# Graph network layer: which engine tells TensorE that a gathered slot is full, and who is told that it was read

## The reference

```
x  = layernorm(x + gcn(x, W, b) + t_emb @ Wt + bt)      # layer 0
h  = relu(mean_over_edges(x[src]) @ Wl1.T + x @ Wr1.T + b1)   # layer 1
y  = mean_over_edges(h[src]) @ Wl2.T + h @ Wr2.T + b2         # layer 2
out = layernorm(x + y)
# gcn: sum over edges of x[src] scaled by 1/sqrt(degree) on both sides, then @ W
# mean_over_edges: segment_sum(msg, dst) / max(count, 1)
```

## Time and profile before

| | |
|---|---|
| three runs | 3864.66, 3865.3 (median), 3870.44 us |
| the profiled execution | 3868.88 us, span of its trace 3867.1 us |
| PE busy | 3067.6 us (79%) |
| POOL busy | 2257.4 us (58%) |
| DVE busy | 1094.8 us (28%) |
| ACT busy | 503.1 us (13%) |
| mean granted clock of TensorE | 0.916 |
| moved by DMA | 1102.52 MB, 285 GB/s over the span |

### The profile page before, as it was taken

One profiled execution on the slowest core, in us unless ns is written; L12 is line 12 of the kernel. 1 busy time (PEld: TensorE's weight loads), 2 busy tenths in 40 slices (PEclk: granted clock), 3 DMA queues, 4 the chain that ended last, 5 costly groups with the idle time before them and its releaser, 6 DMA issues.

```text
span 3867.1 us, 52767 instructions
## 1 busy us (share of the span) xinstructions
PE 3067.6 (79%) x11711; PEld 1400.9 (36%) x12104; DVE 1094.8 (28%) x1877; ACT 503.1 (13%) x1048; POOL 2257.4 (58%) x2367
## 2 busy tenths in 40 slices
PE   7156667778888878788989978886778889988888
PEld 7012223333333333333444433342334344433333
DVE  8701112222333431112222323332122222222222
ACT  0500000111112220000111111111000111111112
POOL 0066666666666636666666666654666666666663
PEclk9988878888899989899999989998889999999999
DMA  5587788888999968888889999987888888888785
GB/s 170 218 301 273 267 274 289 297 305 308 321 323 324 328 244 286 279 282 277 298 309 309 319 328 321 318 311 262 282 278 284 272 281 278 285 280 280 270 279 192
DMA packets 278572, 1102.52 MB, mean 285 GB/s; under 512 B 53626, under 2 KB 55196, under 8 KB 278514
## 3 DMA queue, kind: packets, MB, share of 16 engines
q0 software_dynamic: 187680, 922.63, 69.3%
q10 hardware_dynamic: 64638, 137.22, 10.0%
q1 hardware_dynamic: 26228, 42.34, 3.1%
HBM read 1003.75 MB, written 99.06 MB: 285 GB/s over the span
## 4 chain that ended last, share of the span: by engine, by line
PE 44%; another core or an unknown queue 20%; issue 19%; ACTq 6%; DVE 3%; ACT 3%; DMA 3%; POOL 2%; DVEq 0%; SPq 0%; POOLq 0%
PE sum_ps L1187 27%; PE root_ps L1195 8%; PE prod_ps L1195 7%; POOL raw L457 2%; DMA raw<-table,idx_ring 1%; ACTq L249 1%; PE selfT_ps L1209 1%; PE aggT_ps L1173 1%; ACT selfT L931 1%; ACTq L969 1%; DMA table<-stage 1%; DVE left_of L643 1%; DVE stage L635 1%; ACTq L272 1%
## 5 line engine op out<-in xcount | busy, mean ns | idle before, releaser
L457 POOL DMA_INDIRECT raw<-table,idx_ring x2346 | 2248.0, 958 | 1483.8 <-issue 834.8
L1187 PE MATMUL sum_ps<-raw,oh 128*128 128x512 bf16 x6682 | 1718.1, 402 | 516.4 <-issue 463.6
L1187 PEld LDWEIGHTS sum_ps<-raw,oh 128*128 128x128 bf16 x7038 | 696.1, 102 | 1434.3 <-issue 778.6
L765 DVE TENSOR_TENSOR oh<-iota_ps,dst_rel 128x1280 bf16<-128x1280 f32 x237 | 352.9, 1489 | 1438.5 <-remote 684.2
L1195 PE MATMUL prod_ps<-W,aggT 128*128 128x512 f32 x1176 | 547.4, 607 | 20.9 <-issue 11.8
L1195 PE MATMUL root_ps<-W,selfT 128*128 128x512 f32 x800 | 400.6, 644 | 72.3 <-issue 69.1
L1195 PEld LDWEIGHTS prod_ps<-W,aggT 128*128 128x128 f32 x1176 | 230.3, 197 | 265.9 <-issue 247.4
L887 ACT ACTIVATE aggT<-aggT_ps 128x512 f32<-128x512 f32 x147 | 87.7, 597 | 1827.0 <-remote 1359.9
L1187 PE MATMUL sum_ps<-raw,oh_next 128*128 128x512 bf16 x847 | 229.8, 401 | 37.7 <-issue 26.8
L1195 PEld LDWEIGHTS root_ps<-W,selfT 128*128 128x128 f32 x800 | 160.6, 206 | 270.2 <-issue 258.9
L924 ACT ACTIVATE selfT<-selfT_ps 128x512 f32<-128x512 f32 x100 | 59.7, 597 | 1004.3 <-remote 644.6
(11 more groups left out here) (149 smaller groups left out, 1156.5 us busy)
## 6 DMA issues: line engine op xcount, KB each, us to landing
raw<-table,idx_ring POOLq DMA_INDIRECT x2346
table<-planes ACTq DMA_DIRECT2D x89, 384.0 KB
selfbuf<-rows ACTq DMA_DIRECT2D x104, 256.0 KB
selfbuf<-table ACTq DMA_DIRECT2D x50, 384.0 KB
table<-stage SPq DMA_DIRECT2D x7, 2688.0 KB, 8.3
rows<-X ACTq DMA_DIRECT2D x49, 256.0 KB
X<-rows ACTq DMA_DIRECT2D x49, 256.0 KB
X<-in_x SPq DMA_DIRECT2D x6, 2048.0 KB
```

The source lines that it names most:

```text
L457: nc.gpsimd.indirect_dma_start(out=raw[:, n, j, :], out_offset=None, in_=tables[L][:, :], in_offset=bass.IndirectOffsetOnAxis(ap=idx_ring[ ...
L765: v.tensor_tensor(oh[:, which * HR:(which + 1) * HR, :, :].rearrange("p n j e -> p (n j) e"), iota_ps[:, 0:P].unsqueeze(1).to_broadcast([P ...
L1187: last = mm(bank, of[:, j, :], raw[:, n, j, p * D:(p + 1) * D], start=fresh, stop=False, skip_group_check=True)
```

## The change

`gathered`, `pe_done` and SP's relay are gone. PE waits for `slot_full[n]` itself. In place of `pe_done` there are ten semaphores `slot_read[n]`, one for each slot, each raised by the last matmul on that slot; POOL waits for its slot's, DVE for that of the last slot of the half block. `oh_made` now counts half blocks, and PE waits for it in slots 0 and 5 alone. ACT's wait before it copies row numbers is for `slot_read[9]` (the tenth slot of the block was read) where it was for `gathered` (it has landed). With the relay gone, SP's three later loads stand right behind each other, each with the wait that it had.

```diff
+        slot_read = [sem(f"slot_read{n}") for n in range(SLOTS)]
+        def fills(n, L):
+            return L * (NBLK + (n == 0))
...
-                def landed(blk, n):
-                    fills = NBLK + 1 if n == 0 else NBLK
-                    sp.wait_ge(slot_full[n], blk * (16 * CH) + 16 * CH * (fills * L + 1))
-                    sp.sem_inc(S["gathered"], 1)
-                with sp.Fori(0, ROOTS_DONE) as blk:
-                    for n in range(SLOTS):
-                        landed(blk, n)
                 if L == 1:
                     sp.wait_ge(S["root_ready"], T + 2)
                     load_weights(1, wr2t, "wr_loaded")
-                with sp.Fori(ROOTS_DONE, NBLK) as blk:
-                    for n in range(SLOTS):
-                        landed(blk, n)
-                landed(NBLK, 0)
...
-                        pool.wait_ge(S["pe_done"], blk * SLOTS + (REAL * L + n + 1))
+                        pool.wait_ge(slot_read[n], blk + (fills(n, L) + 1))
...
-                def half_block(which, cols, done):
-                    dve.wait_ge(S["pe_done"], done)
+                def half_block(which, cols, read, times):
+                    dve.wait_ge(read, times)
...
-                        ALU.is_equal).then_inc(S["oh_made"], HR)
+                        ALU.is_equal).then_inc(S["oh_made"], 1)
...
-                                   b * SLOTS + (REAL * L + (half + 2) * HR))
+                                   slot_read[(SLOTS - 1, HR - 1)[half]], b + (fills(1, L) + half + 1))
...
-                    act.wait_ge(S["gathered"], b * SLOTS + (REAL * L + SLOTS))
+                    act.wait_ge(slot_read[SLOTS - 1], b + (fills(1, L) + 2))
                     next_indices(b % 2, (b + 2) % (NBLK + 1))
...
-                def group(g, n, first, end):
-                    pe.wait_ge(S["oh_made"], g + (HR * (NW + 1) * L + 1))
-                    pe.wait_ge(S["gathered"], g + (REAL * L + 1))
+                def group(b, n, first, end):
+                    if n % HR == 0:
+                        pe.wait_ge(S["oh_made"], b * (SLOTS // HR) + ((NW + 1) * L + n // HR + 1))
+                    pe.wait_ge(slot_full[n], b * (16 * CH) + 16 * CH * (fills(n, L) + 1))
                     with pe.If(end > first):
                         add_rows(sums_of(L, first + 1), oh[:, n, :, :], n, False)
...
-                           skip_group_check=True).then_inc(S["pe_done"], 1)
+                           skip_group_check=True).then_inc(slot_read[n], 1)
                     with pe.Else():
-                        add_rows(sums_of(L, first + 1), oh[:, n, :, :], n, False).then_inc(S["pe_done"], 1)
+                        add_rows(sums_of(L, first + 1), oh[:, n, :, :], n, False).then_inc(slot_read[n], 1)
```

More of the change, by code:

```diff
@@ L44, in gnn_resnorm @@
     assert STORE_LAG == FIN_LAG + 3 and ENDS == T - 4
-    ROOTS_DONE = 28
-    assert ROOTS_DONE * SLOTS // HR > T + 1 + 2 * SLOTS // HR
     NL = 3
@@ L186, in gnn_resnorm @@
             total_ps rows_loaded rows_cast src_ps dst_ps tabs_made loads_done bias_ps b0_made b0_all_ps bias_made x_biased ended_made
-            high_made left_made middle_made staged stage_stored0 stage_stored1 zero_stored wl_loaded wr_loaded chain oh_made gathered high_ready split_step planes_ready planes_stored
-            pe_done self_loaded sum_ready agg_ready aggT_done aggT_ready prod_ready prod_read next_made next_used
+            high_made left_made middle_made staged stage_stored0 stage_stored1 zero_stored wl_loaded wr_loaded chain oh_made high_ready split_step planes_ready planes_stored
+            self_loaded sum_ready agg_ready aggT_done aggT_ready prod_ready prod_read next_made next_used
             selfT_done selfT_ready root_ready root_added root_taken
@@ L780, in groups @@
                         half_block(1 - half, bass.ds(b * (SLOTS * CH) + (half + 1) * HR * CH, HR * CH),
-                                   b * SLOTS + (REAL * L + (half + 2) * HR))
-                half_block(0, slice(0, HR * CH), REAL * L + SLOTS)
+                                   slot_read[(SLOTS - 1, HR - 1)[half]], b + (fills(1, L) + half + 1))
+                half_block(0, slice(0, HR * CH), slot_read[0], fills(0, L) + 1)
                 with dve.Fori(0, NBLK) as b:
@@ L942, in high_plane @@
                 elif t1 == ENDS + L:
-                    act.wait_ge(S["pe_done"], REAL * (L + 1) + SLOTS)
+                    act.wait_ge(slot_read[0], fills(0, L + 1) + 1)
                 if L == 0:
@@ L1016, in _ @@
                 each(act, ends[0], ends[1], lambda t1: tile_end(L, t1))
-                act.wait_ge(S["gathered"], REAL * (L + 1))
+                act.wait_ge(slot_read[0], fills(0, L + 1) + 1)
                 next_indices(NBLK % 2, 1)
@@ L1085, in _ @@
             pe.sem_inc(S["root_ready"], 1)
-            pe.sem_inc(S["pe_done"], SLOTS)
+            for n in range(SLOTS):
+                pe.sem_inc(slot_read[n], 1)
             pe.sem_inc(S["next_used"], 1)
@@ L1229, in groups @@
                             each(pe, rounds[n // HR], rounds[n // HR + 1], lambda r: own_rows(L, r), T + 1)
-                        group(b * SLOTS + n, n, ends[n], ends[n + 1])
-                def group(g, n, first, end):
-                    pe.wait_ge(S["oh_made"], g + (HR * (NW + 1) * L + 1))
-                    pe.wait_ge(S["gathered"], g + (REAL * L + 1))
+                        group(b, n, ends[n], ends[n + 1])
+                def group(b, n, first, end):
+                    if n % HR == 0:
+                        pe.wait_ge(S["oh_made"], b * (SLOTS // HR) + ((NW + 1) * L + n // HR + 1))
+                    pe.wait_ge(slot_full[n], b * (16 * CH) + 16 * CH * (fills(n, L) + 1))
                     with pe.If(end > first):
@@ L1249, in _ @@
                 ends = ended_before(mybir.EngineType.PE, TAIL_GROUP, 1)
-                group(TAIL_GROUP, 0, ends[0], ends[1])
+                group(NBLK, 0, ends[0], ends[1])
                 weigh(L, T - 1)
```

## The result

The changed kernel took 3849.27 us in the median of 6 runs (3841.09 to 3855.38), the kernel before on the same chip 3870.29 (3864.66 to 3874.42): a ratio of 0.9945, interval 0.9927 to 0.9962. That is 21 us faster (15 to 28); foretold were 35.

The account below looks back on a forecast made before the run. The bound was taken to be POOL standing, waiting for PE's late word. Terms 0 + 0 - 35 + 0 = -35 took the profiled 3868.9 us to 3834, for a median 3830 us; range 3768 to 3897.

Parts of the forecast that it names:

- The bound: POOL's gathers: speed is set by how often and long POOL stands waiting for PE's word, about 535 us.
- The mechanism: PE: something fills up with executed instructions, some 150 before it slows; 14 instead of 16 a plain slot gives more room.
- The term of -35: PE's instruction count: fewer slow steps and shorter POOL stalls, -35 us, between 0 and 90 us gained.
- signs that were to show it right: Fewer lone 0.70 us loads, more loads before slowing, layer 0 clock above 0.87, POOL waits below 608 us, slots 2.95-3.00 us.
- The relay: SP's 1173 waits with an add removed: 0 us, range 0 to -13, from PE's waits that SP ended.
- POOL's register operation: POOL loses one register operation a slot, beside a 0.95 us gather: 0, within 35 us either way.
- POOL and DVE hear no earlier: POOL and DVE wait for slot_read[n], the same matmul's end as with pe_done, no less late: 0.
- The rival: ACT becomes late: 1.1 us a block delays PE's sum, 3929 us without the gain, 3894 with it; chance 0.20.
- More than the floor: SP's and POOL's removed instructions leave room too, so stalls become rarer: 90 us, 3775 or a little below; chance 0.12.
- The floor of ten slots: POOL in sparse parts: ten slots at 2.5 us and a stall of up to 4.5 us, 2.95 us a slot.
- Nothing moves: POOL's stalls depend on ten slots and landed gathers, both unchanged; removed work was beside other work: 3865 us; chance 0.23.
- latency on the path: PE's shorter instruction path and the relay's delay both count, 180 and 13 us: 3672 us; chance 0.03.

Follow-up runs that it names:

- first set: The first four follow-up kernels, run on one chip, where the kernel before took 3831.6 us (median).
- two more: Changed kernel with two more sequencer instructions on PE ahead of eight of each ten slots: 3823.61 us, 0.9974 of the kernel before.
- one load: Changed kernel with one weight load shared by a chunk's three matmuls instead of three loads: 3769.52 us, 0.9844 of the kernel before.
- six more: Changed kernel with six more sequencer instructions on PE ahead of every slot: 3889.31 us, 1.0152 of the kernel before.
- slot_read alone: Kernel before with only the ten slot_read semaphores in place of pe_done, relay and ACT's wait kept: 3869.39 us, 0.9987 of the kernel before.
- first two sets: The first eight follow-up kernels, four to a chip, where the kernel before took 3831.6 and 3873.9 us (median).
- third set: The last four follow-up kernels, run on another chip, where the kernel before took 3326.1 us (median).

## Why the prediction was right or wrong

**The bound** was read rightly: the change's effect lies in POOL's stalls, 23.5 us of 27.7, and in every pair of the first set the spans and stalls move together (two more to one load: 55.6 and 60.1 us; two more to six more: 65.1 and 51.5).

**The mechanism** was right in kind: PE's slow steps come after a number of executed instructions, words come late, and instructions hidden beside matmuls have a price. It failed in two steps. The first is "if 53 to 61 loads are what PE gets through before it slows, that is some 150 instructions, and the same room now holds 10% more slots". Such a sum doesn't hold: with six more instructions PE slows after some 60 loads and matmuls and 44 to 48 sequencer instructions, 104 to 108 together, where the kernel before came to some 145. Loads and matmuls have a room of some 110, the sequencer one of some 40, and the change took nothing from the first. The second is the way to time, "5.6 to 9.8 us of slow steps spared, where a stretch ends slow": slow steps were hardly what POOL waited for, since the matmul itself was late in 22 of 220 stalls, for 28.7 of 569.8 us. The term of -35 came out at some -10: the ratio with two more instructions lies 0.27% above the changed kernel.

Of the signs that were to show it right, most failed. The lone loads did not become fewer (477 steps for 383), PE did no more loads between a restart and a slow stretch, the clock of layer 0 stayed at 0.87, and slots came under 3.00 us in layer 0 alone. POOL's stalls did shrink, 577.7 to 554.2 us. The sequencer's slow instructions went instead, for which the prediction named no sign. That the total still fell not far from the forecast is partly luck: more than half of the gain comes from parts that the sum had at 0.

**The relay**, term 0 with a bound of -13, is worth some 10 us. The size fits the bound but not its reason, which was PE's waits for SP's word: the cost is there when nobody waits for SP, and more SP instructions cost more.

**POOL's register operation**, 0 within 35, is worth at most the 5 us of slot_read alone. The three parts, 10, 10 and 5, make 25 where 21 were measured; their intervals, 4 to 6 us each way, allow this.

**POOL and DVE hear no earlier**: right. DVE's longest waits remained, 1078.6 us in 87 times on "remote", the longest 30.4. By the tail of about 26 ns per add of the Trainium skill ("TensorE: Matmul & The Clock Gate", "The cost: per-tile semaphore tail") no such wait could come about. In the first two sets and the pair itself the traces contradict the rule as a full account (in the median stall the word took 5 to 10 us); on the third set's chip, where it took 0.84 us, nothing speaks against it. The sum would have been 0 by it, and was not.

**ACT.** Its copy of row numbers is now late by PE's word:

```profile
ACT idx_ring L862 <- remote: 491.9, 37, 52.8
ACT idx_ring L862 <- PE sum_ps L1177: 120.5, 25, 32.2
```

612 us of waits, and still PE waits for ACT's sum 7.9 us in all, where it was 9.9. The rival needed tens of microseconds there, so this row speaks against it; no run isolates it. The prediction also let the copy hide because it is "for ten slots later". That is not so: the copy waits until slot 9 of a block was read, and POOL may start the block that uses it when PE has read one slot more. It did no harm: POOL started a block within 1.2 us of the copy's end 6 times before and 5 times after, and stood there for 7 us before and 1 us after.

**"More than the floor"** rested on instructions of all engines counting together. SP's do, at a lower price, so its premise was half true, and its 90 us far off. The floor of ten slots was not tested. "Nothing moves" is excluded by the interval, twice; "latency on the path" by its 3672 us.

**What stays open**: what it is that fills and empties at 0.70 us a step. The runs show one limit for PE's loads and matmuls, one for its sequencer, one for SP, and a price across engines. The Trainium skill has a path of this shape ("NOTIFIC — the notification-queue block"): the records of an engine's control flow and of its datapath are separate classes, each with a route of its own, though by convention both routes end in one queue ("The producer-side routing registers (in the TPB, not here)"). When a queue of that path is full, it drops the new record, writes over the oldest or stalls whoever feeds it, as it is set ("Overflow: three behaviours, one of which stalls the engine"). The two limits on PE, the steps on an SP that nobody waits for and the lost records of adds agree with that; no run here shows that it is this path.

So the strongest rival stands untested: the recording of the profile may itself be what costs the time, and then all prices here are prices of recorded executions. The timed executions are listed with a span and a granted clock as the profiled ones are, and none is known to have left no records. A run without recording would settle it. Nor is it shown that a limit of DMA throughput starts the slowness: chips that differ in throughput differ in lost records too, and no run changes one of them alone.

## What to carry to other kernels

Pair each long wait with the instruction that should have ended it, and see when that one ended: here it had ended some 8 us before, and the names of releasers alone did not show it. Where a DMA queue is kept full and a word comes late like this, count executed instructions for each queue (loads and matmuls; sequencer; other engines), from a restart to the first lone step, and cut those of the queue that fills first: a weight load that repeats the last one, a register operation, a relay. Add harmless instructions to one engine to find its price before rewriting for it. And compare chips: on the one where words were in time, some 10000 instructions fewer gained 9 us. Before rewriting a kernel for such a price, time it once without recording, if that can be had; it was not done here.

## What the runs showed of the hardware that was not expected

- An idle engine's instructions, waited for by nobody, slow the kernel: 3 to 6 ns each on SP; PE's own cost 4.5 to 11 ns each, though matmuls cover them.
- 0.70 us a step is the same for PE's loads, PE's sequencer and SP, while the counts before it differ: about 110, 40 to 48, and 24.
- The add that a matmul carries can arrive long after the matmul: a median of 7.7 us before POOL's stalls on one chip, 0.84 us on another.
- Where this happens, records are lost: 9,465 to 12,732 of 37,536 adds of landings stand in the traces, against 37,529 or more on the chip without it.
- Matmuls may follow each other on one weight load: 5280 loads fewer gave the same matmuls and 1.0% less than the changed kernel.
- The same kernel took 3326 us on one chip and 3832 to 3874 on others, 15.2 to 16.5% more, and what an instruction costs differs with it.
- A memset between POOL's gathers costs 0.76 us, three and a half times its own 0.22.
